# Four routed tiles worked early, from the counts of ten token tiles, and the rest of the slots listed by the experts' size

## The reference

```python
h = patches @ W.T + b                                   # 2048 x 768 -> 2048 x 192
h = h + attn(layernorm(h))                              # causal, rotary, 12 heads
x = layernorm(h); t = rmsnorm(x) * norm_scale
g = t @ gate_w.T + gate_b                               # 16 experts
top_vals, top_idx = top_k(g, 4); route_w = softmax(top_vals)
# for each token and each of its 4 experts e:
a = swiglu(t @ mlp1_w[e].T + mlp1_b[e])                 # 192 -> 768 -> 384
y = a @ mlp2_w[e].T + mlp2_b[e]                         # 384 -> 192
h = h + x + sum of route_w * y
```

## Time and profile before

| | us |
|---|---|
| median of three runs | 492.59 |
| the profiled execution | 492.28 |
| its span | 490.5 |
| TensorE busy | 436.2 (89%) |
| VectorE busy | 292.7 (60%) |
| ScalarE busy | 313.7 (64%) |
| GpSimd busy | 238.7 (49%) |
| token steps, first product of step 21's ranks | to 188.9 |
| last scatter landed | 200.1 |
| first product of a routed first layer | 204.9 |
| last product | 476.1 |

### The profile page before, as it was taken

How to read it: one execution, slowest core, us unless ns; L and a number is a source line. 1 busy time by engine, 2 the same in 40 slices (tenths; PEclk the granted TensorE clock), 3 DMA queues, 4 the chain that set the end, 5 groups by cost and what they waited for, 6 DMA issues and landing times.

```text
span 490.5 us, 14416 instructions
## 1 busy us (share of the span) xinstructions
PE 436.2 (89%) x3877; PEld 385.4 (79%) x3878; DVE 292.7 (60%) x992; ACT 313.7 (64%) x816; POOL 238.7 (49%) x285
## 2 busy tenths in 40 slices
PE   3589999999999666699999999999999999999980
PEld 3366777786776454499999999999999999999970
DVE  0357789888889747055555555555555556555550
ACT  1057877887787732277667776667766677666730
POOL 2113367877777667103336545344454445444453
PEclk9999999999999655699999999999999999999995
DMA  7766457757793112233335434333443444332332
GB/s 223 189 186 175 141 147 217 207 167 208 186 277 106 71 63 104 81 90 62 60 54 77 61 61 70 61 52 57 68 68 59 59 59 68 61 42 27 33 34 24
DMA packets 42106, 49.72 MB, mean 101 GB/s; under 512 B 6387, under 2 KB 33507, under 8 KB 42052
## 3 DMA queue, kind: packets, MB, share of 16 engines
q1 hardware_dynamic: 27604, 34.35, 26.2%
q0 software_dynamic: 14448, 14.72, 19.3%
HBM read 30.82 MB, written 18.23 MB: 100 GB/s over the span
## 4 chain that ended last, share of the span: by engine, by line
PE 66%; DVE 13%; issue 8%; POOL 6%; DMA 3%; SPq 2%; ACT 1%; POOLq 1%; DVEq 0%; ACTq 0%
PE bank L591 23%; PE bank L613 15%; PE bank L599 13%; PE bank L571 4%; POOL routed_rows L1129 3%; PE bank L421 3%; PE bank L437 2%; PE bank L415 2%; PE bank L438 2%; PE bank L460 1%; DMA b_sb<-b 1%; DVE sc L833 1%; DVE stats L885 1%; POOL p_pair L1158 1%; DVE xn L800 1%
## 5 line engine op out<-in xcount | busy, mean ns | idle before, releaser
L1203 POOL DMA_INDIRECT out_rows<-x_sb,row_to x79 | 123.5, 1563 | 162.3 <-DMA out_rows<-x_sb,row_to 76.2
L591 PE MATMUL bank<-rT,w_now 128*128 128x128 f32 x948 | 124.0, 281 | 0.3 <-ACT rT L636 0.3
L591 PEld LDWEIGHTS bank<-rT,w_now 128*128 128x128 f32 x948 | 115.1, 193 | 5.2 <-ACT rT L636 0.5
L722 ACT ACTIVATE k_spread<-bank,w_now 128x128 f32<-128x128 f32 x237 | 70.0, 372 | 59.3 <-PE bank L599 59.3
L636 ACT ACTIVATE w_now<-w_sb 128x1158 f32 x79 | 92.3, 1170 | 18.7 <-issue 13.2
L1068 DVE TENSOR_TENSOR v_sb<-bank,w_now 128x384 f32<-128x384 f32 x79 | 44.0, 557 | 88.8 <-PE bank L599 69.0
L613 PE MATMUL bank<-w_sb,p_spread 128*128 x474 | 83.9, 327 | 0.1
L1129 POOL DMA_INDIRECT routed_rows<-packet,row_i x64 | 64.1, 1001 | 30.4 <-PE bank L481 16.1
L613 PEld LDWEIGHTS bank<-w_sb,p_spread 128*128 128x128 f32 x474 | 76.1, 190 | 0.5 <-issue 0.4
L1081 DVE SCALAR_TENSOR_TENSOR p_spread<-k_spread,v_sb 128x384 f32<-128x384 f32 x79 | 44.1, 559 | 34.4 <-ACT k_spread L722 30.8
L599 PE MATMUL bank<-rT,w_now 64*128 64x128 f32 x948 | 64.3, 282 | 0.0
(11 more groups left out here) (185 smaller groups left out, 582.8 us busy)
## 6 DMA issues: line engine op xcount, KB each, us to landing
x_sb<-patches SPq DMA_DIRECT2D x16, 384.0 KB, 3.5
w_sb<-w SPq DMA_DIRECT2D x32, 192.0 KB
w_sb<-w SPq DMA_DIRECT2D x16, 288.0 KB
w_sb<-w SPq DMA_DIRECT2D x64, 48.0 KB
wtok_sb<-routed_rows SPq DMA_DIRECT2D x25, 106.0 KB, 2.0
routed_rows<-zero_row SPq DMA_DIRECT2D x17, 106.0 KB
out_rows<-h SPq DMA_DIRECT2D x16, 96.0 KB
out_rows<-x_sb,row_to POOLq DMA_INDIRECT x79, 3.5
```

The costliest lines, as they stand in the source:

```text
L591: last = mm(dst[:, c * P:(c + 1) * P], w[:, a:a + P], t[:, part, :], start=(start and c == 0), stop=(not start and c == ICH - 1))
L722: last = nc.scalar.activation(gate_act[b][:, a:a + P], ps_glu[b][:, a:a + P], ACT.Silu, bias=w1_now[b][:, GLU_B + c:GLU_B + c + 1], scale= ...
L1203: G.indirect_dma_start(out=out, out_offset=bass.IndirectOffsetOnAxis(ap=row_to[:, b % NY:b % NY + 1].bitcast(U32), axis=0), in_=y_out[b % ...
```

## The change

A list of four early slots is made from the counts of the first ten token tiles. Only whole tiles of an expert are taken, from the first experts on. The counts come from one more product at token tile 10's ranks (step 16), eight small operations of VectorE follow in step 17, ten in step 18, and TensorE turns the columns in step 18. SyncE loads the early rows after the stores of two base tiles. The biases of the first layer are turned and written in steps 18 and 19. ScalarE copies two experts' weights in step 19 and the turned rows in step 20; TensorE turns the first two slots' rows at the end of step 19, does half of slot 0's first layer at the end of step 20, and its other half and slot 1's in step 21 ahead of the last bias product. Slots 2 and 3 follow, with the turning of the final list between them, then four second layers. The pairs' loop begins with slot 4. Some PSUM results move to other banks (`bias_of`, `ranks_of`), the warming products are gone.

The final list has 75 slots (`FINAL`). It has 29 operations instead of 23, three of them over 16 x 16 numbers, since the experts are now ordered by their remaining rows: empty slots first, then the smallest expert, the largest last. The output buffers are eight instead of four (`NY`). Four of the heads are cleared by GpSimd (`clear_head`) in steps 2 to 5, so that the `added` semaphores start from 16 (`ADDS_FROM`).

```diff
-TABLE_STEPS = 23
+EARLY, EARLY_TILES = 4, 10
+FINAL = SLOTS - EARLY
+TABLE_STEPS, EARLY_STEPS, EARLY_SOON = 29, 18, 8
...
-        NY = 4
+        NY = 8
...
@@ SyncE
-            for e in range(EXPERTS + 1):
+            for e in range(ADDS, EXPERTS + 1):
...
+            sp.wait_ge(early_ready, 1)
+            sp.wait_ge(s["embedded"], TILES)
+            for buf in range(PACKETS):
+                sp.wait_ge(scattered[buf], 16 * TOPK * ((EARLY_TILES + PACKETS - 1 - buf) // PACKETS))
+            for j in range(EARLY):
+                load_rows(j, j)
...
@@ TensorE
+                if t == EARLY_TILES:
+                    mm(ps_full, ones_bf[:], chosen_before[:], start=True, stop=True).then_inc(early_counted, 1)
...
+                    if tile(5) == TILES - 1:
+                        bank_free(("base_full", TILES - 2))
...
+                if n == TILES + 2:
+                    bank_free(("k_spread_ready", TILES))
+                    turn(ps_b1, b1_sb[:], ident[0:2 * ICH * EXPERTS, 0:2 * ICH * EXPERTS]).then_inc(b1_turned, 1)
...
+                if n == TILES + 2:
+                    pe.wait_ge(early_step, EARLY_STEPS)
+                    for i in range(4):
+                        last = mm(ps_etab[:, i * EARLY:(i + 1) * EARLY], of_early[0:EARLY, i:i + 1], ident[0:EARLY, 0:EARLY],
+                                  start=True, stop=True)
+                    last.then_inc(early_turned, 1)
...
+                    if tile(6) == TILES - 1:
+                        first_end(0, 0)
+                        bank_free(("top_i_ready", TILES))
+                        first_layer(1, 1, False)
                     experts_bias(tile(6))
...
+                if n == TILES + 3:
+                    pe.wait_ge(early_ready, 1)
+                    pe.wait_ge(setup_dve, 5)
+                    pe.wait_ge(experts_in, 16 * LOADS_E * EXPERTS)
+                    turn_early(0)
+                if n == TILES + 4:
+                    bank_free(("place_ready", TILES - 2), ("base_full", TILES - 3))
+                    first_begin(0, 0)
...
+            turn_early(1)
+            first_layer(2, 2, True)
...
-            for i in range(WARM):
-                mm(banks[0][:, 0:INNER], ident, h0[:, i:i + 2, :].rearrange("p a d -> p (a d)"), start=True, stop=True)
...
+            first_layer(3, 3, False)
             pe.wait_ge(s["base_full"], TILES)
+            second_early(0)
+            second_early(1)
...
@@ ScalarE
+                if n == TILES + 3:
+                    act.wait_ge(early_ready, 1)
+                    act.wait_ge(setup_dve, 5)
+                    act.wait_ge(experts_in, 16 * LOADS_E * EXPERTS)
+                    experts = experts_early(0)
+                    for j in range(2):
+                        copy_w1(j, j, experts[j])
+                if n == TILES + 4:
+                    turned_early(0)
...
+            gate(0, 0)
+            experts = experts_early(0) + experts_early(1)
+            copy_w1(2, 2, experts[2])
+            turned_early(1)
+            gate(1, 1)
+            copy_w1(3, 3, experts[3])
+            for j in range(EARLY):
+                note_weight(j, j, experts[j])
+            gate(2, 2)
+            gate(3, 3)
...
@@ VectorE
+                if n == TILES + 1:
+                    early_counts()
+                if n == TILES + 2:
+                    early_table()
+                if n == TILES + 3:
+                    first_biases()
...
+            linear(0, 0)
             dve.wait_ge(counted, 1)
...
+            tab(4, V.tensor_tensor, above, key[:].unsqueeze(1).to_broadcast(pee), key[:].unsqueeze(2).to_broadcast(pee), ALU.is_ge)
+            tab(6, V.tensor_tensor, above_n, above, ntile[:].unsqueeze(1).to_broadcast(pee), ALU.mult)
+            tab(7, V.tensor_reduce, tend[:], above_n, AX_X, ALU.add)
...
             add_bias(TILES - 1)
+            linear(1, 1)
+            product(0, 0)
+            product(1, 1)
             dve.wait_ge(table_turned, 1)
...
+            linear(2, 2)
+            product(2, 2)
+            linear(3, 3)
+            weigh(0, 0)
+            product(3, 3)
+            for j in range(1, EARLY):
+                weigh(j, j)
...
@@ GpSimd
+                if 2 <= n < 2 + ADDS:
+                    clear_head(n - 2)
```

More of the change, by code:

```diff
@@ L296, in written_out @@
                      lambda k, back=0: min(max(n - back - k + 1, 0), tiles), n)
-            for n in range(first):
+            for n in range(begin, first):
                 written_out(n)
@@ L382, in _ @@
             sp.wait_ge(table_ready, 1)
[L384 to L391 removed]
+            for j in range(EARLY, NX):
                 load_rows(j, j)
@@ new lines, in first_rest @@
+            def first_rest(j, buf, start):
+                pe.wait_ge(r["rT_ready"], j + 1)
+                pe.wait_ge(r["w1_ready"], j + 1)
+                wait(pe, r["gate_ready"], j - 1)
+                wait(pe, r["lin_ready"], j - 1)
+                w, t, half = w1_now[buf % 2], rT[buf % 2], P // 2
+                parts = (ps_glu[buf % 2], ps_lin[buf % 2])
+                for c in range(ICH):
+                    for part, dst in enumerate(parts):
+                        k = half * (1 - part)
+                        last = mm(dst[:, c * P:(c + 1) * P], w[k:k + half, REST + c * P:REST + (c + 1) * P],
+                                  t[k:k + half, 1 - part, :],
+                                  start=(start and c == 0), stop=(not start and c == ICH - 1))
+                return last
@@ new lines, in expert_of, with turn_early @@
+            def expert_of(j):
+                return pe.value_load(table_i[0:1, 0, bass.ds(j, 1)], min_val=0, max_val=EXPERTS - 1)
+            def turn_early(pair):
+                for j in (2 * pair, 2 * pair + 1):
+                    pe.wait_ge(rows_in[j], 16)
+                    wait(pe, r["rT_ready"], 2 * pair)
+                    for c in range(2):
+                        a = c * (DIM - P)
+                        last = turn(ps_rT_early[j % 2][:, c, :], rows[j][:, a:a + P], ident)
+                    last.then_inc(r["rows_turned"], 1)
@@ L485, in _, with second_early @@
+            def second_early(pair):
+                experts = [expert_of(j) for j in (2 * pair, 2 * pair + 1)]
+                for j, expert in zip((2 * pair, 2 * pair + 1), experts):
+                    if j == 1:
+                        pe.wait_ge(table_ready, 1)
+                        pe.wait_ge(pad_to_ready, 1)
+                    second_layer(j, j, expert)
             pe.wait_ge(wtok_in, 16)
@@ new lines, in _, with tab @@
+            unrolled(STAGES, TILES, step)
+            made = [0]
+            def tab(needs, op, *args):
+                if needs:
+                    dve.wait_ge(table_step, needs)
+                op(*args).then_inc(table_step, 1)
+                made[0] += 1
+            column = [of_tile[:, i:i + 1] for i in range(11)]
+            pee = [P, EXPERTS, EXPERTS]
+            linear(0, 0)
+            dve.wait_ge(counted, 1)
+            tab(0, V.scalar_tensor_tensor, cnt_i[:], ps_cnt_late, float(P - 1), taken[:, 0:EXPERTS], ALU.add, ALU.subtract)
```

485 lines of the change are left out of this document (283 added, 202 removed).

## The result

The changed kernel took 478.63 us, the median of four runs (476.85 to 482.16); the kernel before took 492.49 beside it (four runs, 491.99 to 493.91). The ratio is 0.9695, 95% interval 0.9646 to 0.9744.

What follows compares the result with a forecast made beforehand. TensorE was taken to bound the routed stage, with latency chains in the token drain and waiting adds at the end around it. 492.28 - 10.4 - 4.3 = 477.6, 477.9 on the median's scale, stated as 478.0; 8-in-10 range 474.5 to 483.5.

Steps and rivals of the forecast that it cites:

- Step 17: Token pass 17: eight small VectorE operations before tile 13's attention sum leave about 0.55 us on the chain (0 to 1.5).
- Steps 18 and 19: Token passes 18 and 19: added work mostly in idle time; 0.2 us (0 to 0.8) in 18, nothing in 19.
- rival D: Early rows come late and their transposes hold tile 15's token work; 495 us at 22 us late; chance 0.04.
- Step 20 to the restart: Token pass 20 to the routed loop's restart: early slots fill TensorE's waits and warm-up; slot 4 at 210.4, worth 10.4 us.
- half clock until about 195.5: TensorE's clock in the drain: half until about 195.5 us, full after it.
- ScalarE's reads: After slot 0's gate: ScalarE reads four expert numbers in 3.0 us; TensorE waits 0.9 us ahead of slot 2.
- rival C: Drain: expert reads cost little and the clock is up by 192; restart at 208.0, 475.5 us; chance 0.09.
- rival A: Drain: clock stays at half until the list is made; restart at 213.6, 481.2 us; chance 0.20.
- The table: VectorE's final list in pass 21: 29 operations take 4.4 us, ready at 199.3, covered by slot 2.
- Rule on short idles: Skill's rule: short idles between product groups can make TensorE's clock fall and rise repeatedly; the new stretch has them at 198.6.
- Order of experts: End of the routed loop: ending with eight tiles of expert 2 removes an add's wait, worth 4.3 us (0 to 5.4).
- Buffers: Loop start: ten waiting adds fall 9 us behind; eight output buffers hold 27 us, so nothing; four would be near the limit.

Runs made afterwards that it cites:

- experiment 9: The changed kernel unedited, a third time, on another chip: 477.33 us, ratio 0.9664.
- experiment 1: The changed kernel unedited, run again on another chip: 484.94 us, ratio 0.9734.
- experiment 4: The changed kernel with useless TensorE products added ahead of the ranks and the weight turning in steps 17 to 19: 486.12 us, ratio 0.9735.
- experiments 2: The changed kernel with experts of the final list taken by index again, early slots kept: 489.24 us, ratio 0.9808.
- 8: The changed kernel with the order of experts turned round, largest first: 485.35 us, ratio 0.982.
- experiments 3: The changed kernel with GpSimd's two list reads ahead of its waits and one stop less: 482.38 us, ratio 0.967.
- 10: Repeat of the changed kernel with GpSimd's list reads ahead of its waits and one stop less: 479.38 us, ratio 0.9705.
- experiment 6: The kernel before with only its list ordered by size, no early slots, four output buffers: 492.93 us, ratio 0.9971.
- 7: The changed kernel with four output buffers instead of eight: 479.59 us, ratio 0.9695.
- experiment 5: The kernel before, unedited, profiled again on another chip: 497.86 us, one run.
- experiment 11: The changed kernel with GpSimd's list reads ahead of its waits, plus ScalarE's four expert reads ahead of the first gate: 476.67 us, ratio 0.9672.

## Why the prediction was right, step by step

- **Step 17**: 0.29 us, predicted 0.55. The sum moved by 1.71 from 163.51, 1.42 of it the late start.
- **Steps 18 and 19**: the twelve scatters start at 185.59, on before's axis (1.42 earlier) 184.2, where 184.4 was predicted. They end at 199.80 against 197.67, 2.13 later, of which 0.7 by the change (0.75 to 1 predicted). The early rows came in time (183.95), so rival D did not occur; its slack was real, the idle 1.71 remains.
- **Step 20 to the restart**: slot 4 starts at 208.42, on before's axis 207.0, not 210.4. The failed step is the clock's: "half clock until about 195.5", and it was full from about 192.7, on that axis 191.3. Slot 1's first layer then ends at 194.6 on that axis and not at 197.2, 2.6 of the miss of 3.4. About 1.7 of the 2.6 is the clock: the rest of slot 0's first layer and slot 1's take 3.1 us together, 4.8 predicted. The other 0.9 was there by 191.5, the end of tile 15's weights (192.4 predicted): the ranks come 0.5 us sooner than I had them and the group is shorter. Most of what is left of the miss is ScalarE's reads: 3.0 us allowed, 1.3 measured, and they end just as slot 1's products do. This is rival C (restart at 208.0), and rival A fell. How early the clock rises is in part luck: in experiment 9, the same kernel, it rises at 193.3 on that axis, and the early part is 1.3 us longer. The 0.95 of the earlier trace rows that the prediction reads as a share of time is the mean of the granted clock in that window; nothing in the sum hangs on it. The table took 4.2 us (194.77 to 199.0; 4.4 predicted). The list was copied at 201.68, on before's axis 200.3 and not 203.7. So it does not release slot 4's rows, as I had it: the last scatter, 199.80 plus the 2.39 of the earlier trace rows, lands at 202.2, and after's rows of slot 4 were issued at 203.12. It cost nothing, since slot 4's transposes then waited for TensorE's second layers, not for rows.
- **Rule on short idles** (the Trainium skill, TensorE: Matmul & The Clock Gate, "A second HAM failure mode"): after's clock stayed at 1.00 from 194 on with idles of 0.56 and 0.26 us in it. The clock did not go down and up there: what the section describes did not occur in this stretch. It fell in experiments 1 and 4, but after longer gaps: 2.82 us in experiment 4, and in experiment 1 the stall (0.84 in 195 to 200 us, then 0.66 in 200 to 205, TensorE busy 3.15 us of the first five).
- **Order of experts**: 2.5 us, 4.3 predicted. The mechanism is right (experiments 2, 8). The mis-sized term is the price of one wait: I took the whole 4.26 us from 474.90 to 479.16 away, but an add that does not wait still starts 1.86 us behind the one before it, so the wait costs 4.26 - 1.86 = 2.40. The prediction let expert 0's three adds go at 474.90, 476.76 and 478.62, and the first of these times already belongs to another add, that of slot 75. They would go at 476.76, 478.62 and 480.48, a tail of 3.3 us; after has 3.21. The tail that remains is set by what stands ahead of a row of adds. In before (GpSimd's and VectorE's timelines) slot 74's:

```profile
470.33 0.41 DVE L1091 TENSOR_SCALAR x_sb<-bank,row_w 128x192 f32<-128x192 f32 x1
...
473.05 1.55 POOL L1203 DMA_INDIRECT out_rows<-x_sb,row_to  x1 [1.28 <-issue]
```

and in after:

```profile
458.75 0.41 DVE L1131 TENSOR_SCALAR x_sb<-bank,row_w 128x192 f32<-128x192 f32 x1
```

Its add goes at 461.15, 2.0 us behind the weighing's end at 459.16 (2.3 in before), and in both kernels GpSimd reads two numbers of the list and stops twice between. Four more adds at 1.86 follow, so the last is at 468.61. With one stop less and the reads ahead the tail is 0.74 less (experiments 3, 10).
- **Buffers**: "near the limit" with four holds: 2.0 us of TensorE lost in experiment 6's windows, 0.85 in 7's, none in after; 2.1 us in the whole of 7. With eight, the predicted "nothing" holds.
- **The start**: not in the prediction, and not the change. TensorE's clock was at half from about 12 us in the profile of after (0.50 in 12 to 16 and in 16 to 20 us) and at full in that of before: tile 1's embedding took 3.68 us and 2.58. But experiment 5, an unchanged before, starts 4.3 us later than its first profile, and experiment 11, which has every added setup operation, reaches tile 14's embedding at 135.60, before 135.91. So the added constants and zero rows cost nothing visible.

The total was right by cancelling, and that is luck: 2.6 us more gained early, 1.8 less in the tail and 1.4 lost at the start add up to 0.6 us less than predicted. The sum's own range (476 to 480.5) was about as wide as one of these errors.

## What to carry to other kernels

When a pipeline drains through latencies, work that is already known to be needed is worth most inside the waits: it fills them (2.2 to 3.5 us here for the first layers of two slots). Adds that chain on one queue should end with the longest independent run. What an order pays there is, for each wait removed, the spacing with the wait less the spacing without it (4.26 - 1.86), not the whole spacing. Before a difference of 1% is explained, subtract the start: measure from a late landmark that both kernels have.

## What was not expected of the hardware

The same kernel reached the same landmark at 135.9 or 140.2 us (before), and at 137.3, 138.7 and 140.0 (after), and TensorE's clock in the first 40 us differs with it. Windows of experiment 11 and of experiment 9:

```profile
20.00:24.00 4.00, 2.82 (x14) 2.53 (x12) 1.63 (x5) 0.00 (x0) 0.44 (x2) 1.00 0.17 44
```

```profile
20.00:24.00 4.00, 4.00 (x15) 3.75 (x13) 1.64 (x5) 0.00 (x0) 0.00 (x0) 0.59 0.21 60
```

Same work, clock 1.00 and 0.59, and tile 14's embedding at 135.60 and 140.01. Seven runs of one unedited kernel, 6.2 us apart, divide by their mean clock (0.96 and 0.94); only one of them has a profile, so how much of the 6.2 us is the start is not shown. In the drain the clock's rise differs alike: 55.4 us behind tile 14's embedding in after and 57.4 in experiment 9. What decides it was not found.
